# Attention with 16 wavelengths: VectorE makes the exponential of a whole key tile from integer bits, weights come by quarters, values are copied first

## The reference

```python
cos_pm = jnp.cos(phase_modulators)                 # [16 wavelengths, 16 heads]
def wl_step(acc, wl):
    cpm, iw = wl
    m = cpm[None, :, None, None]
    Qw = Q * m
    Kw = K * m
    scores = jnp.einsum('bhqd,bhkd->bhqk', Qw, Kw) * SCALE
    scores = scores * jnp.cos(KERR * scores * scores)
    attn = jax.nn.softmax(scores, axis=-1)
    out = jnp.einsum('bhqk,bhkd->bhqd', attn, V)
    return (acc + out * iw, None)
...
x = _layernorm(x + _L0_attn_ref(x, ...), axis=-1)
x = _layernorm(x + _L0_ffn_ref(x, ...), axis=-1)   # router, top 2 of 8 experts plus a skip gate, gelu
```

## Time and profile before

| what | value |
|---|---|
| median of 3 runs | 7535.9 us (7534.82 to 7537.15) |
| the profiled execution, device time | 7540.05 us |
| its span, first to last instruction | 7538.4 us |
| ScalarE busy | 7184.6 us (95%) |
| TensorE busy | 5560.1 us (74%) |
| VectorE busy | 5456.0 us (72%) |
| GpSimd busy | 44.4 us (1%) |
| mean granted TensorE clock | 0.939 of 2.4 GHz |

### The profile page before, as it was taken

One profiled execution on the slowest core, in us unless ns is written; L12 is line 12 of the kernel. 1 busy time (PEld: TensorE's weight loads), 2 busy tenths in 40 slices (PEclk: granted clock), 3 DMA queues, 4 the chain that ended last, 5 costly groups with the idle time before them and its releaser, 6 DMA issues.

```text
span 7538.4 us, 124074 instructions
## 1 busy us (share of the span) xinstructions
PE 5560.1 (74%) x43972; PEld 2013.9 (27%) x43972; DVE 5456.0 (72%) x9488; ACT 7184.6 (95%) x2227; POOL 44.4 (1%) x112
## 2 busy tenths in 40 slices
PE   6767767677777777777777777777777777777777
PEld 2222222222222222222222222222222222222225
DVE  4767677767777777777777777777777777777763
...
GB/s 57 4 4 4 2 4 4 3 3 9 28 25 28 17 26 23 19 28 19 29 28 16 25 28 16 26 28 16 28 30 17 26 27 14 28 17 26 27 12 34
DMA packets 40422, 151.80 MB, mean 20 GB/s; under 512 B 7969, under 2 KB 26273, under 8 KB 33441
## 3 DMA queue, kind: packets, MB, share of 16 engines
...
q0 software_dynamic: 768, 1.57, 0.1%
...
## 4 chain that ended last, share of the span: by engine, by line
ACT 44%; issue 29%; PE 12%; DVE 8%; ACTq 6%; DMA 1%; DVEq 0%; POOLq 0%; SPq 0%; POOL 0%
ACT ring L522 43%; PE pv L593 8%; ACTq L517 4%; DVE scores L724 2%; DMA out<-tile_out 1%; DVE vprobs L747 1%; ACTq L518 1%; DVE tile_z L810 1%; PE sc L1042 1%; PE tr L1050 1%; PE sc L648 1%; DVE qt L718 0%; DVE tile_small L360 0%; DVE tile_small L359 0%; DVE tile_small L361 0%
## 5 line engine op out<-in xcount | busy, mean ns | idle before, releaser
L522 ACT ACTIVATE ring<-scores 128x4096 f32<-128x4096 f32 (+3 forms) x2048 | 6979.3, 3497 | 144.5 <-PE pv L593 109.3
L593 PE MATMUL pv<-ring,vh 128*32 128x512 f32 x31744 | 4010.8, 635 | 1702.1 <-ACT ring L522 1574.4
L593 PEld LDWEIGHTS pv<-ring,vh 128*32 128x32 f32 x31744 | 1003.7, 115 | 4350.8 <-ACT ring L522 2189.0
L754 DVE COPY numer<-pv 128x512 f32<-128x512 f32 x512 | 353.6, 691 | 1067.7 <-PE pv L593 1062.4
L747 DVE SCALAR_TENSOR_TENSOR vprobs<-vprobs,vrest 128x512 f32<-128x512 f32 x1536 | 1063.8, 693 | 52.3
L714 DVE TENSOR_REDUCE rowmax<-sc 128x1 f32<-128x1024 f32 x512 | 602.5, 1219 | 120.8 <-PE sc L556 120.8
L724 DVE COPY scores<-sc 128x1024 f32<-128x1024 f32 (+1 forms) x512 | 601.6, 1217 | 59.0 <-PE sc L575 58.4
L593 PE MATMUL pv<-vprobs,vh 128*32 128x512 f32 x1024 | 530.3, 599 | 0.0
L745 DVE TENSOR_TENSOR vprobs<-vprobs,vrest 128x512 f32<-128x512 f32 x512 | 354.7, 693 | 17.6
L741 DVE SCALAR_TENSOR_TENSOR vrest<-vpower,vrest 128x512 f32<-128x512 f32 x512 | 354.6, 693 | 17.6
L748 DVE SCALAR_TENSOR_TENSOR vprobs<-vprobs,vpower 128x512 f32<-128x512 f32 x512 | 354.5, 692 | 17.4
...
## 6 DMA issues: line engine op xcount, KB each, us to landing
tile_w<-in_L_ffn_w SPq DMA_DIRECT2D x48, 2048.0 KB, 7.6
...
ring<-in_L_ffn_w SPq DMA_DIRECT2D x2, 2048.0 KB, 11.5
...
```

The costliest lines, as they stand in the source:

```text
L522: nc.scalar.activation(ring[:, i % SLOTS, 0:cols], scores[:, bass.ds(n % 2, 1), half * CK:(half + 1) * CK, :].rearrange("p o k s -> p (o k ...
L593: last = nc.tensor.matmul(pv[g * VC:(g + 1) * VC, pair % 2, :], vh[:, buf, half * CK + k, :], probs, start=(half == 0 and k == 0), stop=(h ...
L754: nc.vector.tensor_copy(numer[:, pair, :], pv[:, pair, :]).then_inc(pv_read, 1)
```

## The change

There are three parts.

1. `exponentials` covers the whole last key tile of the pair's second wavelength (128 x 1024 instead of 128 x 512) in seven instructions: the score is scaled by log2(e) x 2^23 and cast to an integer; its exponent bits and its mantissa bits are cut out with bitwise operations, the exponent once as a power of two (`vpower`) and the mantissa as a number from 1 to 2 (`vmant`, kept in a piece of the ring's last slot that ScalarE no longer writes); three two-input operations build a second stream (`vprobs`). The exponential is the sum of the two streams, each with a factor. TensorE adds them: `vlast` holds the values of the last key tile times either factor, and for the two strips of the second wavelength there are two matmuls, one for each stream, in place of one. GpSimd makes `vlast`. ScalarE's fourth chunk of each pair is 128 x 3072 instead of 128 x 3584.
2. `tile_w` holds two quarters of a weight matrix (512 KB each) instead of a whole; SP loads the next quarter when TensorE has used one.
3. In the tile stage GpSimd copies the values of the next heads before it waits for the tile's result.

```diff
 LOG2E = float(np.log2(np.e))
-EXP2 = (0.6931469775987168, 0.24022242084634685, 0.05550733743574262, 0.009671512688178108, 0.0013264727247206184)
-EXP2_LOW = -127.0
-VSTEPS = 10
+EXP2_ALPHA, EXP2_BETA, EXP2_GAMMA = -1.70058876, 14.93555207, 1.54356314
+EXP2_BASE, EXP2_REST = 0.5 * 0.50996422, 0.5 * 0.01353417
+EXPONENT, MANTISSA, ONE = 0x7F800000, 0x007FFFFF, 0x3F800000
+LOWEST = -(2.0 ** 30)
+VSTEPS = 7
 START = 1
...
-        vprobs = sb("vprobs", [P, 2, HALF])
-        vpower = sb("vpower", [P, HALF])
-        vrest = sb("vrest", [P, HALF])
+        vpower = sb("vpower", [P, 2, S])
+        vprobs = sb("vprobs", [P, 2, S])
+        vbits = sb("vbits", [P, S], I32)
+        vmant = ring[:, SLOTS - 1, (CK - 1) * S:CK * S]
+        vlast = sb("vlast", [P, 2, 2, VC])
+        pm_sb = vprobs[:, 1, 0:W * H]
         rowmax = sb("rowmax", [P, KT])
...
-        tile_w = sb("tile_w", [P, NE * F])
+        tile_w = sb("tile_w", [P, 2, WC])
         tile_h = sb("tile_h", [P, NE * F])
...
+            w1_cols, w2_cols = w1.rearrange("d e f -> d (e f)"), w2.rearrange("p e c d -> p (e c d)")
+            def load_weights(sp, cols, k):
+                sp.dma_start(tile_w[:, k % 2, :], cols[:, k * WC:(k + 1) * WC]).then_inc(tile_weights[k % 2], 16)
             def tile_loads(i, ahead, values=None):
...
                 sp.dma_start(tile_att[:, :], att_dram[bass.ds(i, 1)].rearrange("o p e -> p (o e)")).then_inc(tile_in, 16)
-                sp.wait_ge(tile_products, i + START)
-                sp.dma_start(tile_w[:, :], w1.rearrange("d e f -> d (e f)")).then_inc(tile_w1, 16)
+                sp.wait_ge(tile_parts, 4 * i + START)
+                load_weights(sp, w1_cols, 0)
+                load_weights(sp, w1_cols, 1)
                 if ahead:
...
+        def put_values(pool, n, values, buf):
+            nc.gpsimd.tensor_copy(vh[:, buf, :, 0:D], values).then_inc(vh_copied, 1)
+            pool.wait_ge(vh_copied, n + 1)
+            apart(pool)
+            for j, factor in enumerate((EXP2_BASE, EXP2_REST)):
+                last = nc.gpsimd.tensor_scalar(vlast[:, buf, j, 0:D], vh[:, buf, KT - 1, 0:D], factor, None, ALU.mult)
+            last.then_inc(vh_ready, 1)
         def copy_values(pool, n, buf):
...
             pool.wait_ge(slot_free, NCH * (n - 1) + SLOTS)
-            nc.gpsimd.tensor_copy(vh[:, buf, :, 0:D], vv[:, :, bass.ds((n % H) * D, D)]).then_inc(vh_ready, 1)
+            put_values(pool, n, vv[:, :, bass.ds((n % H) * D, D)], buf)
...
             pool.wait_ge(v_loaded, 16)
-            nc.gpsimd.tensor_copy(vh[:, 0, :, 0:D], vv[:, :, 0:D]).then_inc(vh_ready, 1)
-            nc.gpsimd.tensor_copy(vh[:, 1, :, 0:D], vv[:, :, D:2 * D]).then_inc(vh_ready, 1)
+            put_values(pool, 0, vv[:, :, 0:D], 0)
+            put_values(pool, 1, vv[:, :, D:2 * D], 1)
             with pool.Fori(1, FIRST_PAIR) as i:
...
                 copy_values(pool, 2 * i + 1, 1)
-            with pool.Fori(0, PAIRS - FIRST_PAIR) as i:
-                copy_values(pool, 2 * (i + FIRST_PAIR), 0)
+            copy_values(pool, H, 0)
+            def store_tile(i, last=False):
                 copy_values(pool, 2 * (i + FIRST_PAIR) + 1, 1)
+                if not last:
+                    copy_values(pool, 2 * (i + FIRST_PAIR) + 2, 0)
                 pool.wait_ge(tile_done, i + 1)
...
                 pool.sem_inc(tile_out_free, 1)
+            with pool.Fori(0, PAIRS - FIRST_PAIR - 1) as i:
+                store_tile(i)
+            store_tile(PAIRS - FIRST_PAIR - 1, True)
...
-                        cols = CK * S - (HALF if half == 1 and w2 == 1 else 0)
+                        cols = CK * S - (S if half == 1 and w2 == 1 else 0)
                         nc.scalar.activation(ring[:, i % SLOTS, 0:cols],
...
                     col = k * S + qh * HALF
-                    probs = ring[:, 2 * half + w2, col:col + HALF]
-                    if half == 1 and k == CK - 1 and g == G - 1:
-                        pe.wait_ge(vexp_step, VSTEPS * (8 * n + pair + 1))
-                        probs = vprobs[:, pair % 2, :]
-                    last = nc.tensor.matmul(pv[g * VC:(g + 1) * VC, pair % 2, :], vh[:, buf, half * CK + k, :], probs,
+                    sums = pv[g * VC:(g + 1) * VC, pair % 2, :]
+                    if half == 1 and k == CK - 1 and w2 == 1:
+                        continue
+                    last = nc.tensor.matmul(sums, vh[:, buf, half * CK + k, :], ring[:, 2 * half + w2, col:col + HALF],
                                             start=(half == 0 and k == 0), stop=(half == 1 and k == CK - 1))
+            if half == 1:
+                for j, (stream, step) in enumerate(((vpower, 2), (vprobs, VSTEPS))):
+                    pe.wait_ge(vexp_step, VSTEPS * (8 * n + pair) + step)
+                    for qh in range(2):
+                        g = 2 * qh + 1
+                        last = nc.tensor.matmul(pv[g * VC:(g + 1) * VC, pair % 2, :], vlast[:, buf, j, :],
+                                                stream[:, pair % 2, qh * HALF:(qh + 1) * HALF], start=False, stop=(j == 1))
             last.then_inc(slot_free, 2)
...
+            pe.wait_ge(tile_weights[k % 2], 64 * i + 16 * (k // 2 + 1))
             if k == 0:
-                pe.wait_ge(tile_w1, 16 * (i + 1))
                 pe.wait_ge(sc_free, USES * (m + 1))
...
             for j in range(2 * FC):
-                col = (2 * FC * k + j) * P
-                last = nc.tensor.matmul(sc[:, k % 2, j * P:(j + 1) * P], tile_w[:, col:col + P], tile_x1T[:, :], start=True, stop=True)
+                last = nc.tensor.matmul(sc[:, k % 2, j * P:(j + 1) * P], tile_w[:, k % 2, j * P:(j + 1) * P], tile_x1T[:, :], start=True, stop=True)
             last.then_inc(tile_hidden, 1)
...
+            pe.wait_ge(tile_weights[wi % 2], 64 * i + 32 + 16 * (wi // 2 + 1))
             if wi == 0:
-                pe.wait_ge(tile_w2, 16 * (i + 1))
                 pe.wait_ge(tile_gelu, i + 1)
...
                     col = (e * FC + c) * P
-                    last = nc.tensor.matmul(sc[:, 1, e * P:(e + 1) * P], tile_h[:, col:col + P], tile_w[:, col:col + P],
+                    last = nc.tensor.matmul(sc[:, 1, e * P:(e + 1) * P], tile_h[:, col:col + P], tile_w[:, wi % 2, col - wi * WC:col - wi * WC + P],
                                             start=(c == 0), stop=(c == FC - 1))
-            if wi == 3:
-                last.then_inc(tile_products, 1)
+            last.then_inc(tile_parts, 1)
...
             base = VSTEPS * (8 * m + pair)
-            y = scores[:, bass.ds(m % 2, 1), KT - 1, HALF:S].rearrange("p o s -> p (o s)")
-            rest, power, probs = vrest[:, :], vpower[:, :], vprobs[:, pair % 2, :]
+            score = scores[:, bass.ds(m % 2, 1), KT - 1, :].rearrange("p o s -> p (o s)")
+            bits, mant, power, probs = vbits[:, :], vmant, vpower[:, pair % 2, :], vprobs[:, pair % 2, :]
             then = stepper(dve, vexp_step, base, [0])
...
-            then(nc.vector.tensor_scalar(rest, y, scales_log2[:, bass.ds((2 * pair + 1) * H + m % H, 1)], EXP2_LOW, ALU.mult, ALU.max))
-            then(nc.vector.tensor_scalar(power, rest, MAGIC, None, ALU.add))
-            then(nc.vector.scalar_tensor_tensor(rest, power, -MAGIC, rest, ALU.add, ALU.subtract))
-            then(nc.vector.tensor_scalar(power.bitcast(I32), power, -(MAGIC - 127.0), 2.0 ** 23, ALU.add, ALU.mult))
-            then(nc.vector.tensor_scalar(probs, rest, -EXP2[4], EXP2[3], ALU.mult, ALU.add))
-            then(nc.vector.tensor_tensor(probs, probs, rest, ALU.mult))
-            for coefficient in (-EXP2[2], EXP2[1], -EXP2[0]):
-                then(nc.vector.scalar_tensor_tensor(probs, probs, coefficient, rest, ALU.add, ALU.mult))
-            nc.vector.scalar_tensor_tensor(probs, probs, 1.0, power, ALU.add, ALU.mult).then_inc(vexp_step, 1)
+            then(nc.vector.tensor_scalar(bits, score, scales_log2[:, bass.ds((2 * pair + 1) * H + m % H, 1)], LOWEST, ALU.mult, ALU.max))
+            then(nc.vector.tensor_scalar(power.bitcast(I32), bits, EXPONENT, 0x40000000, ALU.bitwise_and, ALU.bitwise_xor))
+            then(nc.vector.tensor_scalar(mant.bitcast(I32), bits, MANTISSA, ONE, ALU.bitwise_and, ALU.bitwise_or))
+            then(nc.vector.tensor_scalar(bits, bits, EXPONENT | MANTISSA, 0x40000000, ALU.bitwise_and, ALU.bitwise_xor))
+            then(nc.vector.scalar_tensor_tensor(probs, mant, EXP2_ALPHA, mant, ALU.add, ALU.mult))
+            then(nc.vector.scalar_tensor_tensor(probs, probs, EXP2_BETA, bits.bitcast(FP32), ALU.add, ALU.mult))
+            nc.vector.scalar_tensor_tensor(probs, mant, EXP2_GAMMA, probs, ALU.add, ALU.mult).then_inc(vexp_step, 1)
...
```

37 lines of the change are left out of this document (23 added, 14 removed).

## The result

| | before | changed |
|---|---|---|
| median | 7537.15 us (5 runs) | 7498.85 us (5 runs) |
| ratio, with its 95% interval | | 0.9946 [0.9932, 0.9961] |
| the profiled execution | 7540.05 us | 7501.78 us |
| ScalarE busy | 7184.6 us | 6970.5 us |
| ScalarE waiting for TensorE | 109.3 us | 284.8 us |

The kernel is 38 us faster; forecast were 203, and the time lies outside the range. ScalarE's two rows explain the sum: 214.1 us less work, 284.8 - 109.3 = 175.5 us more waiting, 38.6 us in all. The forecast had the work right and the waits wrong. One of the five executions of the changed kernel, 7664.72 us at a granted clock of 0.80, is left out of the ratio, as is one of 8468.19 in experiment 16; neither moves its median by more than 0.5 us.

What follows compares the result with a forecast made beforehand. ScalarE was taken to set the time. Against the profiled 7540 us: -221 - 87 + 6 + 81 + 12 + 1 + 5 gives 7337, so 7333 for the median; range for 8 in 10: 7285 to 7460.

Steps and rivals of the forecast that it cites:

- The stop goes at all 23 places: Tile ends: copying values first removes TensorE's wait for GpSimd and so ScalarE's stop, 3.8 us each, 87 us off.
- What is late next at this place is the transposes: Tile ends: transposes waiting for VectorE's copy behind the layer norm come next, giving 24 x 0.25 = 6 us back.
- even the slow 5.97 fits: Tile ends: TensorE can start 6.4 us before ScalarE's slot is wanted, enough even for a first half of 5.97 us.
- plain heads: Heads without tiles: 13.19 us a pair; first halves that run as slowly add 5 us in all.
- ScalarE's chunks: One chunk in four loses 512 columns, 0.431 us each over 512 chunks: 221 us off.
- tile ends: Where one tile ends and the next head starts: 87 us off for GpSimd's wait, 6 us back for late transposes.
- part 1: First part of each tile: longer exponentials and second half make ScalarE stand 4.2 us; net 81 us back.
- behind the Gelu: After TensorE's wait for ScalarE's Gelu: halves come about 0.5 us late, 24 times, 12 us back.
- The dearer end for the last round: TensorE's second half: two more matmuls cost a whole round, 0.91 us, rather than 0.46 by count.
- The rival of slow integer instructions: VectorE's bitwise instructions run at the two-input rate, exponentials take 8.20 us, about 7450 us in all; chance 0.15.
- the one in which VectorE sets the time: Rival: bitwise instructions of 1.6 us or more make VectorE the limit, slower than before; chance 0.04.
- the one in which part 1 doesn't bite: Rival: the tile's chain has slack, the 81 us aren't paid, about 7250 us; chance 0.07.

Runs made afterwards that it cites:

- experiment 16: Changed kernel with TensorE's loop turning at the Gelu wait, router and logits' exponential later, plus a needless 2048-column ScalarE activation in each tile: 7325.96 us, 0.9716.
- experiment 5: Kernel before, with only TensorE's loop over the tiles turning where it waits for the Gelu instead of between two tiles: 7536.67 us, 0.9997.
- experiments 3, 4 and 14: Changed kernel, TensorE's loop over tiles written out (7401.57 us), turning at the Gelu wait (7335.42 us), or turning between parts 1 and 2 of a tile (7402.93 us).

## Why the prediction was wrong

The failed step is "The stop goes at all 23 places", with "What is late next at this place is the transposes". What was late next was the jump of TensorE's own loop. It leaves about 3.4 us of idle time, just less than GpSimd's 4.31, so the wait for GpSimd hid it, and the profile named only the one that came last. (Alone GpSimd's wait is 2.86 us, experiment 5: the jump even made it longer.) The one place of the 23 without a jump is also the one where the stop went, as forecast; experiments 3, 4 and 14, each with the changed kernel's exponentials and weights, remove the other 22. Behind the jump stood a second stop of 0.88 us and a half at the 1.2 GHz level, 6.25 us, which the working had covered with "even the slow 5.97 fits", counted from a start that didn't come. The row that should have warned was the 3.50 of "issue" at the turns of the plain heads, of which one cost before only 0.34 us of ScalarE's time, since nothing else was late there. Why a jump of these loops takes 3 us and more stays open.

Point by point:

| step | forecast | measured |
|---|---|---|
| ScalarE's chunks | -221 | -218 (0.425 us each) |
| tile ends | -87 + 6 | +69: 155.6 us of waits against 86.4 |
| part 1 | +81 | +69: 24 x 3.7, less 20 |
| behind the Gelu | +12 | +5: 9 tiles of 24 |
| pair 6 of part 2 | none | +23: 22 tiles |
| plain heads | +5 | +10: 7 jumps |
| weights by quarters | 0 | no wait |
| bitwise instructions | 689 ns | 694 ns |
| two-input instructions | 1219 ns | 1225 ns |
| TensorE's second half | 4.55 us | 4.49 us |

The tile ends are 150 us off, nearly the whole miss of 165. The second step that failed is smaller: pair 6 of part 2 stood in no term, since VectorE's longer exponential was followed through part 1 alone; its 23 us are nearly made up by part 1 and the Gelu, which came 19 us below their terms. The dearer end for the last round was the right one: 4.49 us are 0.85 more than 3.64. With the rule on column strips (the Trainium skill, "TensorE: Matmul & The Clock Gate", Part 3) the trace agrees: two strips cost 0.85 us, where four cost 0.91. The rival of slow integer instructions is out by 694 ns, the one in which VectorE sets the time by ScalarE's 93%, and the one in which part 1 doesn't bite by the 2.81 + 0.89 us. The forecast of about 7333 would have held with one edit that the change did not have, the turn at the Gelu: 7335. That agreement is partly luck: a tile's time came in steps of 3.4 us, two of the six executions were at 7403 and 7405, and in that kernel other terms cancel (behind the Gelu 0.6 us for 12, part 1 69 for 81, pair 6 of part 2 14 for none, plain heads +12 for 5).
